# Another order of loads and maxima in the first stage of an attention and mixture-of-experts kernel

## The reference

```python
def _fp8_quant_dequant(x):
    amax = jnp.max(jnp.abs(x))
    scale = FP8_E4M3_MAX / jnp.maximum(amax, EPS)
    q = jnp.clip(x * scale, -FP8_E4M3_MAX, FP8_E4M3_MAX).astype(jnp.float8_e4m3fn)
    return q.astype(jnp.float32) / scale

x = x + _L0_xattn_ref(_layernorm(x, axis=-1), ctx_2048, mask_Bx1xS2_ff0)
x = x + _L0_ffn_ref(_layernorm(x, axis=-1), ...)
```

## Time and profile before

| | us |
|---|---|
| median of three runs | 1987.12 |
| lowest and highest run | 1985.38 and 1987.95 |
| the profiled execution | 1987.5 |
| its span in the trace | 1985.9 |
| TensorE busy | 1831.9 (92%) |
| VectorE busy | 1390.6 (70%) |
| ScalarE busy | 864.7 (44%) |

### The profile page before, as it was taken

How to read it: one execution, slowest core, us unless ns; L and a number is a source line. 1 busy time by engine, 2 the same in 40 slices (tenths; PEclk the granted TensorE clock), 3 DMA queues, 4 the chain that set the end, 5 groups by cost and what they waited for, 6 DMA issues and landing times.

```text
span 1985.9 us, 44057 instructions
## 1 busy us (share of the span) xinstructions
PE 1831.9 (92%) x17396; PEld 1398.4 (70%) x17396; DVE 1390.6 (70%) x2509; ACT 864.7 (44%) x1209; POOL 606.0 (31%) x611
## 2 busy tenths in 40 slices
PE   0039999999999999999999999999999999999997
PEld 0018578668667767766866876778888888888886
DVE  5888675576567557557545544588888888888884
ACT  8564221222212212122221121367777777777773
POOL 2100210220220221122022022355655656656552
PEclk9989999999999999999999999999999999999999
DMA  9936534433433443434243244499999999999993
GB/s 377 392 98 198 127 86 96 109 95 86 107 98 75 107 118 68 114 96 95 76 107 75 54 107 125 140 333 356 354 370 356 355 371 354 359 372 349 363 371 78
DMA packets 188301, 395.45 MB, mean 199 GB/s; under 512 B 116304, under 2 KB 120432, under 8 KB 163600
## 3 DMA queue, kind: packets, MB, share of 16 engines
q1 hardware_dynamic: 163184, 334.77, 49.0%
q0 software_dynamic: 23808, 58.81, 13.5%
q10 hardware_dynamic: 1184, 0.15, 0.0%
HBM read 314.79 MB, written 55.35 MB: 186 GB/s over the span
## 4 chain that ended last, share of the span: by engine, by line
PE 84%; issue 3%; DVE 2%; DMA 1%; POOL 1%; SPq 0%; ACT 0%; POOLq 0%; DVEq 0%; ACTq 0%
PE ps L1345 51%; PE ps L1358 15%; PE ps L1531 8%; PE ps L1385 5%; PE ps L1539 2%; PE ps L1421 1%; DVE W L1024 1%; PE ps L1451 1%; DMA xn_rows<-FR 1%; POOL slots L555 1%; DMA FR<-xn_rows,gix 0%; PE ps L1426 0%; PE ps L1457 0%; DMA BIG<-in_sh_down 0%; SPq L467 0%
## 5 line engine op out<-in xcount | busy, mean ns | idle before, releaser
L1345 PE MATMUL ps<-XT,W 128*128 128x256 f16 (+1 forms) x12288 | 1112.4, 253 | 5.0 <-issue 2.5
L1345 PEld LDWEIGHTS ps<-XT,W 128*128 128x128 f16 x12288 | 1025.0, 98 | 90.2 <-issue 15.4
L1289 DVE SCALAR_TENSOR_TENSOR W<-BIG,W 128x2048 f16<-128x2048 f32 x192 | 436.2, 2286 | 64.5 <-ACT W L848 64.5
L848 ACT ACTIVATE W<-BIG 128x2048 f16<-128x2048 f32 x192 | 361.4, 1901 | 0.0
L1358 PE MATMUL ps<-W,HH 128*128 128x512 f16 x1536 | 334.3, 379 | 0.0
L790 ACT ACTIVATE SG<-ps 128x256 f32<-128x256 f32 x128 | 48.9, 382 | 612.5 <-PE ps L1345 612.5
L1358 PEld LDWEIGHTS ps<-W,HH 128*128 128x128 f16 x1536 | 150.3, 98 | 180.8
L257 POOL TENSOR_TENSOR expo<-expo 128x1 f32<-128x1 f32 x159 | 82.1, 516 | 621.2 <-ACT FR L719 267.4
L1203 DVE SCALAR_TENSOR_TENSOR SG<-ps,SG 128x256 f32<-128x256 f32 x128 | 54.3, 424 | 232.7 <-ACT SG L790 232.7
L548 POOL TENSOR_TENSOR rs<-ve,expo 128x1 f32<-128x1 f32 x32 | 17.6, 549 | 565.0 <-DVE ve L1045 565.0
L599 POOL DMA_INDIRECT FR<-xn_rows,gix x64 | 173.0, 2703 | 30.0 <-issue 30.0
(11 more groups left out here) (178 smaller groups left out, 1627.7 us busy)
## 6 DMA issues: line engine op xcount, KB each, us to landing
BIG<-in_w_gate SPq DMA_DIRECT2D x64, 1024.0 KB, 9.0
BIG<-in_w_up SPq DMA_DIRECT2D x64, 1024.0 KB, 7.6
BIG<-in_w_down SPq DMA_DIRECT2D x64, 1024.0 KB, 8.2
X<-in_x SPq DMA_DIRECT2D x16, 1024.0 KB, 5.2
X<-in_mask POOLq DMA_DIRECT2D x16, 1024.0 KB, 8.1
xn_rows<-FR SPq DMA_DIRECT2D x32, 512.0 KB, 3.7
out_rows<-X SPq DMA_DIRECT2D x32, 512.0 KB, 3.6
W<-in_x SPq DMA_DIRECT2D x6, 2048.0 KB, 19.6
```

The source lines that it names most:

```text
L848: ac.activation(dst, stage, ACT.Copy, scale=W_SCALE).then_inc(x_hi, 1)
L1289: ve.scalar_tensor_tensor(out=lo[cut], in0=src, scalar=W_SCALE, in1=hi[cut], op0=ALU.mult, op1=ALU.subtract).then_inc(x_lo, 1)
L1345: ins = te.matmul(out_ps, a[:, k, cols], b[:, k, :], start=n == 0, stop=n == len(steps) - 1)
```

## The change

The tables of loads and maxima have another order, and three lines follow from that:

- x0, x1 and x2 come first without a ctx piece between, then c0 and c1 among x3 and x4, then b0 and b1; b2 and b3 stand ahead of c4 and c5, which are now the last of both tables.
- The two initialising stores are issued behind b3, so ahead of c4, and no longer behind x4. `x_load(0, 0)` keeps its place behind c5, which now is the end of the loop: b2 and b3 no longer stand between it and `x_load(1, 1)`.
- Behind x7 VectorE waits for the maxima of the 12 pieces up to x7, and not for all 14; the wait for 14 stands ahead of the last reduction.
- The row spread that belongs to x's maximum stands behind c4 (it stood behind b2), and the last reduction behind c5 (it stood behind b3).

```diff
-        LOADS = [("x", 0), ("b", 0), ("x", 1), ("x", 2), ("b", 1), ("x", 3), ("c", 0), ("x", 4), ("c", 1), ("x", 5),
-                 ("c", 2), ("x", 6), ("c", 3), ("x", 7), ("c", 4), ("c", 5), ("b", 2), ("b", 3)]
...
+        LOADS = [("x", 0), ("x", 1), ("x", 2), ("c", 0), ("x", 3), ("c", 1), ("x", 4), ("b", 0), ("b", 1), ("x", 5),
+                 ("c", 2), ("x", 6), ("c", 3), ("x", 7), ("b", 2), ("b", 3), ("c", 4), ("c", 5)]
+        PEAKS = [("x", 0), ("x", 1), ("c", 0), ("x", 2), ("c", 1), ("b", 0), ("b", 1), ("x", 3), ("x", 4), ("c", 2),
+                 ("x", 5), ("c", 3), ("x", 6), ("b", 2), ("b", 3), ("x", 7), ("c", 4), ("c", 5)]
...
-                if piece == ("x", 4):
+                if piece == ("b", 3):

                     sp.wait_ge(consts_ready, 2)
                     sp.dma_start(out[T:T + C, :].rearrange("(t p) d -> p t d", p=HC),
...
                 if piece == ("x", XCHUNKS - 1):

-                    dve.wait_ge(p1_done, XCHUNKS + CCHUNKS)
+                    dve.wait_ge(p1_done, p1_freed(piece))
                     dve.wait_ge(x_norm, 1)
...
-                if piece == ("b", 2):
+                if piece == ("c", 4):
                     peak_spread_row(0)
-                if piece == ("b", 3):
+                if piece == ("c", 5):
+                    dve.wait_ge(p1_done, XCHUNKS + CCHUNKS)
                     ch.sync()
```

More of the change, by code:

```diff
@@ L284, in moe_kernel @@
         sw_dram = [sh_gate, sh_up, sh_down]
-        LOADS = [("x", 0), ("b", 0), ("x", 1), ("x", 2), ("b", 1), ("x", 3), ("c", 0), ("x", 4), ("c", 1), ("x", 5),
-                 ("c", 2), ("x", 6), ("c", 3), ("x", 7), ("c", 4), ("c", 5), ("b", 2), ("b", 3)]
-        PEAKS = [("b", 0), ("x", 0), ("x", 1), ("b", 1), ("x", 2), ("c", 0), ("x", 3), ("c", 1), ("x", 4), ("c", 2),
-                 ("x", 5), ("c", 3), ("x", 6), ("c", 4), ("c", 5), ("x", 7), ("b", 2), ("b", 3)]
+        LOADS = [("x", 0), ("x", 1), ("x", 2), ("c", 0), ("x", 3), ("c", 1), ("x", 4), ("b", 0), ("b", 1), ("x", 5),
+                 ("c", 2), ("x", 6), ("c", 3), ("x", 7), ("b", 2), ("b", 3), ("c", 4), ("c", 5)]
+        PEAKS = [("x", 0), ("x", 1), ("c", 0), ("x", 2), ("c", 1), ("b", 0), ("b", 1), ("x", 3), ("x", 4), ("c", 2),
+                 ("x", 5), ("c", 3), ("x", 6), ("b", 2), ("b", 3), ("x", 7), ("c", 4), ("c", 5)]
         RING = [piece for piece in LOADS if piece[0] != "b"]
```

## The result

The changed kernel takes 1983.49 us (median of 20 runs, 1980.91 to 1987.25), the kernel before 1987.56 us in the same series (20 runs, 1985.30 to 1992.81). The ratio is 0.9979, with a 95% interval from 0.9973 to 0.9985: 4.1 us faster.

The account below looks back on a forecast made before the run. TensorE, busy 92% of the span, was taken to bound the kernel, with the load stage setting L719's start. L719 moving from 100.06 to 95.85 us gives -4.2 us on 1987.12: 1982.9 us, range 1980.9 to 1985.5.

Parts of the forecast that it names:

- The stream as a clock: Load stage: pieces land at fixed spacing, 5.12 us per 2 MB piece, 2.56 per b piece, while the stream never runs dry.
- the 1.90 us: Load stream: cost of the two init stores, taken from c0's and c1's landings (12.14 - 10.24).
- The maxima behind c3: VectorE: from c3's landing at 67.2 us it never idles again, so c5's maximum starts at 89.90 us.
- x7's squares: ScalarE: squares end at 81.2 us, first half about 2.3 earlier; VectorE asks at 80.3, so just covered.
- The small steps at the end: From the last maximum's start to L719: 3.81 us before, 5.95 with the wider last piece, so L719 at 95.85.
- SP's wait for x3's maximum: SP queue: c3's load issued at 53.3 us instead of 45.73, with no stream gap and 3 us to spare.
- the stores are ahead of c5 in both orders: Load order: the init stores precede c5 before and after, so c5 lands 5.12 us later, at 89.57.
- All that the change can win is the shift of L719: ScalarE's start at 100.06 us: its shift is all the change can win or lose; gain 4.2 us.
- The first rival: TensorE's clock, restart at L1385: takes or gives back 1.85 us, 1981.1 to 1984.8; chance 0.10 for better by 1 us or more.
- The second rival: Stream runs dry at c3's load, landing 8.1 to 10.7 us late: 1990.7 to 1993.0 us; chance 0.05.
- The third: Shift partly swallowed by VectorE at c3, x7's squares or a later load: 1.5 to 3.5 us left; chance 0.22.
- the fourth: Load stage: same bytes and same maxima, so the order changes nothing, 1987.1 us; chance 0.03.

Follow-up runs that it names:

- e9: The changed kernel itself, run again unedited in the rounds of e10; 1984.53 us, ratio 0.9978 to the kernel before.
- e4: Kernel before with both old tables, only the two stores moved from behind x4 to behind x7; single run 1988.65 us.
- e1: Changed kernel with the old head of both tables (b0, b1 spread among x0 to x3); 1983.51 us, ratio 0.9973 to the kernel before.
- e3: Changed kernel with the old tail of both tables (c4, c5 ahead of b2, b3) and stores behind x4; 1988.63 us, ratio 1.0007 to the kernel before.
- e2: e1 with the two stores back behind x4, so only the tail is changed; 1986.14 us, ratio 0.9992 to the kernel before.
- e8: Changed kernel with the scale of x made behind c4's maximum instead of c5's; 1984.15 us, ratio 0.9973 to the kernel before.
- e10: e8 with x's first rounding steps woven into VectorE's two waits for TensorE; 1982.20 us, ratio 0.9969 to the kernel before.
- e6: Changed kernel with SP issuing c3's load only behind c2's maximum; single run 1989.39 us.
- e7: Changed kernel with SP issuing c3's load only behind x5's maximum; single run 1992.47 us.
- e5: Changed kernel with the two stores back behind x4; ratio 0.9983 to the kernel before.

## Why the prediction was right

The forecast was 4.2 us, the measured gain is 4.1, with an interval of some 3.0 to 5.4 us. The mechanism was right step by step, but that the two numbers lie 0.1 us apart is partly luck: the start that the sum was made for moved by 3.98 us, and the first product by 4.40.

- **The stream as a clock** held: 5.12 us for a piece, 2.56 for a b piece, and 1.90 for the stores place c3 at 67.2; it came at 67.43, and at 67.20 in e9. This 0.2 us is the whole error at the end of the stage (L719 at 96.08, worked out as 95.85), and no more than the scatter. The one weak number is the 1.90 us, read from a single pair of landings: over all profiles the stores cost 1.6 us.
- **The maxima behind c3** held piece by piece: worked out 71.53, 75.91, 80.29, 85.12, 89.90, read 71.77, 76.15, 80.54, 85.37, 90.14. All are 0.24 us later, none drifts. x7's squares were in time, and VectorE waited for nothing.
- **The small steps at the end** (5.95 us) took 96.08 - 90.14 = 5.94 us.
- **SP's wait for x3's maximum**: c3 issued at 53.65 (53.3 forecast), and the stream stayed full. The margin rested on at most 3.9 us of fixed time for a load. The forced cases measure 2.8 us, between that bound and the 2.0 us of the Trainium skill (DMA: Bandwidth & Descriptors, "Anatomy of one DMA"). That section gives its figure for DMAs issued from GpSimd, and these loads are issued from SP.
- **What the prediction said less well** is which edit does what. It wrote that the stores are ahead of c5 in both orders, which reads as if their move were free. In its own sum they were not: c3's landing had them taken off. The runs show that the move is worth 1.6 us under the new tail and nothing under the old one (e4), and that the reordered head, most of the diff's rows, is worth nothing under either (e1, e3). The rest, 2.5 us (e2), is the tail: the new last piece has 4.4 us of maximum behind its landing where the old end had four pieces in a row.
- **"All that the change can win is the shift of L719"** was true of this change, but for 0.4 us. It would not be true of every change: L719 is on the path only by the 1.71 us that VectorE waits ahead of L958 (e8).
- **What it did not see**: behind L719 the new tail wins another 0.42 us. In the three kernels with the old tail (before, e3, e4) VectorE stands idle for 0.53 us in the middle of its rounding, and in none of the nine others. The rows name no other engine for it, and its cause stays open. The kernel before, then the changed kernel:

```profile
119.59 2.29 DVE L961 SCALAR_TENSOR_TENSOR BIG<-W,BIG 128x2048 bf16<-128x2048 f32 x1 [0.53 <-DVE BIG L960]
```

```profile
115.19 2.29 DVE L961 SCALAR_TENSOR_TENSOR BIG<-W,BIG 128x2048 bf16<-128x2048 f32 x1
```

- **The first rival**, TensorE's clock: the price was mis-sized. The first 16 matmuls of L1385 behind the pause were given 1.85 us of loss (5.31 against half of 6.92). Over the twelve profiles they take from 3.63 us (e8, e10) to 6.48 us (the changed kernel), so 0.2 to 3.0 us are lost. The granted clock goes with it. Here are a stretch of the changed kernel, at the lower level (1.2 GHz), and then e8's 16 matmuls with the same stretch, at 2.4 GHz. TensorE had stood idle for 4.85 us ahead of them in the changed kernel and for 3.44 us in e8:

```profile
204.00:207.00 3.00, 3.00 (x9) 1.08 (x8) 1.81 (x6) 0.00 (x0) 0.55 (x1) 0.50 0.00 0
```

```profile
201.85 3.63 PE ps L1386 x16
```

```profile
204.00:207.00 3.00, 3.00 (x15) 1.37 (x14) 2.37 (x6) 0.00 (x0) 0.55 (x1) 1.00 0.00 0
```

  In the changed kernel's own profile this and a slower stretch ahead of it (last section) took back 2.2 of the 4.4 us that the first product had won: L1359 starts 2.16 us earlier than L1358 did (209.98 against 206.82 + 5.31). The medians of 20 runs show the full shift all the same. That such losses fall on both kernels alike would explain it, but is not shown.
- **The second rival** was far off. Its price is real once the stream is dry, its premise is not (e6, e7). Its own figures were also 0.4 to 0.7 us too early: a c3 that is 8.1 to 10.7 us late, with nothing to take it up, puts L719 at 95.85 plus that, 104.0 to 106.6 and not 103.6 to 105.9, and the gain is gone at 4.2 us, not 4.5.
- The third (partly swallowed) and the fourth (nothing) did not happen.

## What to carry to other kernels

When a stage is a load stream with work behind it, find the last landing after which the working engine never pauses: only what is ahead of that landing in the stream, and how much work stands behind it, sets the end. The same move of a store was worth nothing with a pause behind it and its full time without one, so the worth of an edit must be priced in the order in which it will stand. And a start on another engine that lies on the path is worth moving only by the wait that it causes: read that wait (here 1.71 us), and take off what the edit adds to the engine that waits.

## What the runs showed that I had not expected

First, the scatter behind the stage. From L719's start to the first L1385 it took 106.76 us before and 107.42 us in the changed kernel; with the same code behind L719 the other profiles (e1 to e7, e9) have 105.88 (e3) to 107.71 us (e9). In the changed kernel's chain of waits, one store of normalised rows took 11.81 us to land, where it took 11.24:

```profile
153.72 11.81 DMA xn_rows<-FR
```

```profile
157.72 11.24 DMA xn_rows<-FR
```

(the changed kernel, then the kernel before). In the other profiles with that code it took 10.81 (e4) to 12.31 us (e5), and the 16 matmuls behind the restart of TensorE's clock 4.97 (e5) to 6.48 us. So these two places move a single execution by up to 1.5 us each, beside the 4.1 us that the change brings; the 20 runs of the changed kernel lie between 1980.91 and 1987.25 us. Whether they make up all of that scatter is not shown. A gain of this size is seen in one profile only at a place ahead of these two.

Second, a load into an empty queue took 2.8 us beyond its bytes, in both forced cases, while the same load in a full queue took 14 to 25 us from issue to landing (c3 in the changed kernel 13.8, the loads before 16.7 to 24.6). Its issue time says nothing about its landing as long as something is in front of it: c3's load was issued 8 us later than before and landed 1.7 us earlier.
